# Attention scores of a graph network: the gathered source row is added by TensorE, in place of VectorE

## The chip, the cores and the metric

One core of one Trainium2 chip. The metric is the time on the device of one run of the whole program, in microseconds (us); the kernel before has a median of 9190.53 us over three runs. PE is TensorE, DVE is VectorE, ACT is ScalarE, POOL is GpSimd, SP is SyncE.

## What is computed

Four graph layers run one after the other over 3125 nodes with 64 features and 100,000 edges, each followed by a layer norm. The change touches the last, which holds two GATv2 layers (5 heads of 64 channels). Each does, per edge from `src` to `dst`:

```python
xl = (x @ Wl + bl).reshape(n_nodes, H, C)
xr = (x @ Wr + br).reshape(n_nodes, H, C)
e = jax.nn.leaky_relu(xl[src] + xr[dst], NEG_SLOPE)
alpha = jnp.einsum('ehc,hc->eh', e, att)
# then a softmax of alpha over the edges of one dst, and a sum of a * xl[src]
```

Only the first step of a layer, the scores `alpha` (up to terms that the kernel folds into 2 extra channels a head), is concerned here: `xl[src] + xr[dst]`, 330 numbers an edge (5 heads of 66).

## The kernel before

`gat_edges` (L2229) makes the scores. It is called once for each of the two layers.

**Tiles.** The edges are sorted by `dst` and lie in columns of 128. There are 864 columns (784 of edges and 80 spare ones for columns that cross a boundary). `G = 2` columns are a group, `KC = 12` columns a chunk. One turn of the loop does two chunks, so 24 columns or 12 groups, and there are 36 turns.

**Ahead of the loop** (L2334 to L2347 on PE, with ACT, DVE and SP): for each of 25 blocks of 128 nodes, h is transposed and multiplied in f32 by the two weight matrices (L2344, L2345, 330 columns each). The source part goes to `node_rows` in DRAM (330 numbers and the 64 of h, 1576 bytes a row), the destination part, split in three bf16 terms, to `xr3` and then as a whole into `parts` in SBUF.

**In the loop**, each engine runs its own list of instructions and waits on semaphores:

- POOL (L2321 to L2329) gathers the source rows: one indirect DMA for each column, 128 rows, into `rows`, which has 4 slots of 6 columns (3 groups). Before a slot it waits for its indices (`index_in`), for its release by DVE (`used`) and for SP's store of it (`stored`). Each gather raises `got` of its slot.
- SP loads the row numbers for ACT (L2285) and POOL's next indices (L2290), and stores the h part of each slot to `x_src` (L2296), all in one order written out by hand.
- ACT makes the one-hot matrix of a chunk in two operations (L2384, L2387). The second waits until PE has finished the chunk that used the same buffer (`made`), and raises `hot_made`.
- PE (L2350 to L2361) makes the destination part: for each column one bf16 product of the one-hot matrix with `parts`, 330 columns, into one bank of `psZ`. `psZ` has 4 buffers of 2 banks, one buffer a group. PE waits for `prod`, which says that DVE has read the group four back, and raises `made` after a group.
- DVE (L2407 to L2434) does three operations for each group of 2 columns (660 numbers a partition): it adds the gathered source row to psZ, in place (L2416, it waits for `made`, and for `got` at the first group of a slot, and raises `added`); it takes the maximum with 0, times `att`, from psZ into `lz` (L2423, raises `prod`); it sums over the channels (L2429, raises `scored`). The three are staggered: in one pass it adds for group n, multiplies for n - 1 and reduces for n - 2. After the addition of a slot's last group it releases the slot (`used`, L2421). After six groups the sums are copied into `sj` (L2433).

So the order is POOL's gather and PE's product, then DVE's three operations; POOL can be four slots, PE four groups ahead of DVE.

Of the kernel before, what the change touches and what calls it, by code (L numbers as in the profile page):

```python
# [5 lines left out]
P = 128  # L6
# [17 lines left out]
CE = 128  # L24
# [24 lines left out]
ZH = H * ZC  # L49
# [52 lines left out]
class Space:  # L102


    used = {}
# [2125 lines left out]
def gat_edges(nc, g, h, selfs):  # L2231
# [6 lines left out]
    with phase(nc) as s:  # L2238
# [13 lines left out]
        got = [s.pool_sem(g, k) for k in range(SLOTS)]  # L2252
        dve_c, staged, put, parts_in, cleared = (
            s.sem(n) for n in ("dve_c", "staged", "x_put", "parts_in", "cleared"))
        hot_made, made, added, prod, scored, neared = (s.sem(n) for n in ("hot_made", "made", "added", "prod", "scored", "neared"))
        padded, n_turned, n_ready, n_made, n_tab, n_high, n_split = (
            s.sem(n) for n in ("padded", "n_turned", "n_ready", "n_made", "n_tab", "n_high", "n_split"))
        grp = lambda i, n: i * (2 * NG) + (n + 1)
# [6 lines left out]
        with nc.Block() as block:  # L2265
# [66 lines left out]
            def _(pe):  # L2332
# [17 lines left out]
                with pe.Fori(0, NK // 2) as i:  # L2350
                    for n in range(2 * NG):
                        k, m = divmod(n, NG)
                        if m == 0:
                            at = pick((i * 2 + k) * KC)
                            pe.wait_ge(hot_made, i * 2 + k + 3)
                        pe.wait_ge(prod, grp(i, n))
                        for j in range(G):
                            col = m * G + j
                            last = pe.matmul(psZ[:, n % 4, j, 0:ZH], hot[:, k, col * CE:(col + 1) * CE], parts[:, bass.ds(at[col], 1), :].rearrange("p o c -> p (o c)"),  # L2359
                                             start=True, stop=True)  # L2360
                        last.then_inc(made, 1)  # L2361

            @block.scalar
# [26 lines left out]
            def _(v):  # L2390
# [14 lines left out]
                    v.sem_inc(n_split, 1)  # L2405

                def turn(i, last):  # L2407
                    for n in range(2 * NG + 2):
                        if n < 2 * NG:
                            k, m = divmod(n, NG)  # L2410
                            v.wait_ge(made, grp(i, n) + 2 * NG)
                            slot, at = divmod(n, GS)
                            if at == 0:
                                v.wait_ge(got[slot], i * (16 * KS) + 16 * KS)
                            here = psZ[:, n % 4, :, 0:ZH]
                            v.tensor_tensor(here, here, rows[:, slot, at * G:(at + 1) * G, 0:ZH], ALU.add).then_inc(added, 1)  # L2416
                        if 1 <= n <= 2 * NG:
                            q = n - 1
                            v.wait_ge(added, grp(i, q))
                            if q % GS == GS - 1:  # L2420
                                v.sem_inc(used[q // GS], 1)  # L2421
                            v.wait_ge(scored, grp(i, q))
                            v.scalar_tensor_tensor(lz[:, q % 2], psZ[:, q % 4, :, 0:ZH], 0.0,  # L2423
                                                   att.unsqueeze(1).to_broadcast([P, G, ZH]), ALU.max, ALU.mult).then_inc(prod, 1)
                        if n >= 2:
                            q = n - 2
                            k, m = divmod(q, NG)
                            v.wait_ge(prod, grp(i, q) + 4)
                            v.tensor_reduce(sc[:, k, m * G:(m + 1) * G, :], lz[:, q % 2].rearrange("p g (h c) -> p g h c", c=ZC),  # L2429
                                            X, ALU.add).then_inc(scored, 1)  # L2430
                            if m == NG - 1:
                                v.wait_ge(scored, grp(i, q) + 2)
                                c.link(v.tensor_copy(g.sj[:, :, bass.ds((i * 2 + k) * KC, KC)], sc[:, k].rearrange("p j h -> p h j")))  # L2433
# [517 lines left out]
```

## Time and profile before

| | |
|---|---|
| median of 3 runs | 9190.53 us (9164.67 to 9205.76) |
| profiled execution, time | 9157.66 us |
| its span, from the first instruction to the last | 9156.1 us |
| granted TensorE clock over the span | 0.608 |
| share of the span busy: PE, DVE, ACT, POOL | 42%, 58%, 27%, 41% |
| the loop, each of two layers | 1248 us |

The profile is of one execution. Busy time is that of an engine's operations; handing out instructions and waiting are not in it. An operation's row names the line, the output and inputs, the count, the busy time in all and the mean of one in ns, then the engine's idle time just before it and what ended that. "Issue" is time in which an engine waited for nothing that the profile shows. A timeline row has the start in us from the span's start, the length, and in square brackets the idle time before it.

### The profile page before, as it was taken

The numbers are of one execution on the slowest core, as the hardware profiler recorded it, in microseconds if no ns is written. First come the engines' busy times: TensorE is split into PE (matmuls) and PEld (weight loads), VectorE is DVE, ScalarE is ACT, GpSimd is POOL, SyncE is SP. The second block draws the span as 40 slices with busy tenths as digits, with TensorE's granted clock in tenths as the row PEclk, the third lists the DMA queues.
The fourth block names the chain that finished last, engine by engine and source line by source line (L and its number), as shares of the span: only waits on it lengthen the run. The fifth ranks groups of instructions, "written<-read, shape, count | busy, mean of one in ns | idle before, by whom it ended". The sixth has DMA issues, their size and how long they took to land. (4 is left out here: it accounts for less than half of the span.)

```text
span 9156.1 us, 102588 instructions
## 1 busy us (share of the span) xinstructions
PE 3846.7 (42%) x24601; PEld 3085.2 (34%) x24602; DVE 5285.9 (58%) x8989; ACT 2454.3 (27%) x3870; POOL 3780.2 (41%) x4315
## 2 busy tenths in 40 slices
PE   5455555520017881444443232222249522222196
PEld 2444444520017881333333210000048300000186
DVE  5454445569742112444444468888856588888675
ACT  4333333321622221433333221111112111111121
POOL 4444444400020004444444236666625166666261
PEclk8555555555558995666666555555579555555596
DMA  7565556677737881222222366666645477666462
GB/s 291 152 186 174 170 179 186 184 212 194 284 67 266 293 281 52 82 83 80 93 80 81 44 179 183 184 183 184 171 99 132 128 183 185 182 183 183 107 139 69
DMA packets 1551900, 1462.17 MB, mean 160 GB/s; under 512 B 1296593, under 2 KB 1344365, under 8 KB 1535296
## 3 DMA queue, kind: packets, MB, share of 16 engines
q1 hardware_dynamic: 966152, 807.40, 28.8%
q0 software_dynamic: 175712, 462.09, 19.3%
q10 hardware_dynamic: 409944, 191.70, 7.4%
q8 instruction: 28, 0.46, 0.0%
q14 instruction: 64, 0.52, 0.0%
HBM read 1078.30 MB, written 381.40 MB: 159 GB/s over the span
## 5 line engine op out<-in xcount | busy, mean ns | idle before, releaser
L2328 POOL DMA_INDIRECT rows_p<-node_rows,stage_i x1728 | 1637.9, 948 | 1090.7 <-issue 842.8
L2359 PE MATMUL psZ<-parts_r,hot_t 126*128 x1728 | 629.5, 468 | 1948.7 <-issue 966.3
L2359 PEld LDWEIGHTS psZ<-parts_r,hot_t 126*128 126x128 bf16 x1728 | 181.0, 105 | 2398.1 <-issue 2378.1
L715 PE MATMUL psP<-window,pair_hot 128*128 x3136 | 725.6, 420 | 579.4 <-issue 349.9
L790 DVE SCALAR_TENSOR_TENSOR pair_run<-pair_run,same_c,psP 128x64 f32<-128x64 f32 x1568 | 440.1, 281 | 871.9 <-remote 743.4
L2416 DVE TENSOR_TENSOR psZ<-psZ,rows_p 128x660 f32<-128x660 f32 x864 | 724.7, 846 | 357.7 <-issue 236.5
L715 PEld LDWEIGHTS psP<-window,pair_hot 128*128 128x128 f32 x3136 | 690.8, 329 | 626.7 <-issue 626.7
L257 POOL DMA_INDIRECT rows_s<-hpx,stage_i x784 | 748.5, 955 | 264.7 <-issue 242.7
L257 POOL DMA_INDIRECT both<-table,stage_i x784 | 742.9, 948 | 264.0 <-issue 242.6
L2423 DVE SCALAR_TENSOR_TENSOR lz<-psZ,att 128x660 f32<-128x660 f32 x864 | 723.0, 837 | 95.1 <-issue 69.1
L2429 DVE TENSOR_REDUCE sc<-lz 128x10 f32<-128x660 f32 x864 | 711.9, 831 | 59.4 <-issue 45.1
L2685 PE MATMUL ps_steps<-A,xs 128*65 128x125 f32 x5184 | 574.6, 271 | 145.1 <-DMA xs<-x_src 81.0
L2685 PEld LDWEIGHTS ps_steps<-A,xs 128*65 128x65 f32 x5184 | 558.8, 137 | 160.6 <-issue 153.0
L2384 ACT ACTIVATE near<-locs,third 126x1536 bf16<-126x1536 bf16 x144 | 226.8, 1575 | 1289.6 <-DMA locs<-loc_rows 827.6
L1573 PE MATMUL psY<-parts,tile 128*125 128x192 bf16 x5700 | 516.9, 248 | 112.3 <-DVE parts L1613 97.5
L1938 DVE SCALAR_TENSOR_TENSOR gate<-psZ,la 128x256 f32<-128x256 f32 x196 | 82.9, 423 | 803.1 <-ACT la L1877 655.1
L1573 PEld LDWEIGHTS psY<-parts,tile 128*125 128x125 bf16 x5700 | 484.5, 138 | 117.8 <-DVE parts L1613 98.1
L603 ACT ACTIVATE tile<-psA 128x500 bf16<-128x500 f32 x399 | 203.4, 558 | 979.4 <-remote 640.3
L2704 DVE TENSOR_TENSOR A<-hotw,aw 128x3000 f32<-128x3000 f32 x108 | 354.5, 3283 | 172.1 <-PE ps_steps L2685 171.7
L2659 POOL TENSOR_TENSOR acc<-acc,part_w 65x125 f32 x648 | 316.2, 488 | 282.9 <-ACT part_w L2623 189.1
L2387 ACT ACTIVATE hot_t<-near 126x1536 bf16<-126x1536 bf16 x144 | 213.5, 1483 | 793.0 <-issue 584.4
L1835 PE MATMUL psZ<-b,ones 128*128 128x512 bf16 x196 | 94.3, 481 | 720.4 <-ACT bothT L1867 661.1
(523 smaller groups left out, 8016.2 us busy)
## 6 DMA issues: line engine op xcount, KB each, us to landing
tile<-adj SPq DMA_DIRECT2D x228, 781.2 KB, 4.8
x_src<-rows_p SPq DMA_DIRECT2D x288, 192.0 KB
xs<-x_src SPq DMA_DIRECT2D x432, 128.0 KB, 3.1
locs<-loc_rows SPq DMA_DIRECT2D x144, 378.0 KB
hpx<-stage ACTq DMA_DIRECT2D x25, 2048.0 KB
pair_loc<-pair_locs SPq DMA_DIRECT2D x28, 1792.0 KB
window<-hpx SPq DMA_DIRECT2D x196, 256.0 KB
dst_runs<-pair_run SPq DMA_DIRECT2D x28, 1792.0 KB
```

The costliest lines, as they stand in the source:

```text
L257: pool.indirect_dma_start(buf[:, k, j, 0:width] if width == buf.shape[3] else buf[:, k, j, D:2 * D], None, table, bass.IndirectOffsetOnAxi ...
L715: last = pe.matmul(psP[:, n % 2, j * D:(j + 1) * D], hot[:, n % 2, j * CE:(j + 1) * CE], window[:, n % 2, bass.ds(rel[j], 1), :].rearrange ...
L790: v.scalar_tensor_tensor(run[:, k, at, :], run[:, k, at - 1, :] if at else run[:, 1 - k, PC - 1, :], same[:, k, at:at + 1], psP[:, n % 2, ...
L1573: last = pe.matmul(psY[0:TC, k, 0:3 * D], tile[:, k, b, :], parts[:, b].rearrange("p n c -> p (n c)"), start=b == 0, stop=b == NB - 1)
L2328: pool.indirect_dma_start(rows[:, k, j, :], None, g.node_rows, bass.IndirectOffsetOnAxis(stage[:, k, j:j + 1], 0)).then_inc(got[k], 16)
L2359: last = pe.matmul(psZ[:, n % 4, j, 0:ZH], hot[:, k, col * CE:(col + 1) * CE], parts[:, bass.ds(at[col], 1), :].rearrange("p o c -> p (o c)"),
L2416: v.tensor_tensor(here, here, rows[:, slot, at * G:(at + 1) * G, 0:ZH], ALU.add).then_inc(added, 1)
L2423: v.scalar_tensor_tensor(lz[:, q % 2], psZ[:, q % 4, :, 0:ZH], 0.0, att.unsqueeze(1).to_broadcast([P, G, ZH]), ALU.max, ALU.mult).then_inc ...
L2429: v.tensor_reduce(sc[:, k, m * G:(m + 1) * G, :], lz[:, q % 2].rearrange("p g (h c) -> p g h c", c=ZC), X, ALU.add).then_inc(scored, 1)
L2659: pool.tensor_tensor(here, here, part[:, k, j * WC:(j + 1) * WC], ALU.add).then_inc(added, 1)
L2685: last = pe.matmul(slot(k, j), xs[:, k, j, e, 0:D + 1], A[:, k, j * EG + e, :], start=e == 0, stop=e == EG - 1)
L2704: v.tensor_tensor(A[:, k].rearrange("p f (n h) -> p f n h", h=H), hot[:, k].unsqueeze(3).to_broadcast([P, U * EG, WN, H]), aw[:, k].rearra ...
```

## The change

The identity matrix `ident` (128 x 128, f32) is there already. PE now does two products into the same bank for each column: the bf16 one, which starts the sum, and an f32 product of the identity with the gathered row, 330 columns, which adds to it. PE waits for the slot's gathers, in DVE's place. DVE's addition and the semaphore `added` go. DVE's list for a group is then: wait for `made`, release the slot if the group was its last, wait for `scored`, multiply, and reduce for the group before. The stagger is one group less deep.

```diff
-        hot_made, made, added, prod, scored, neared = (s.sem(n) for n in ("hot_made", "made", "added", "prod", "scored", "neared"))
+        hot_made, made, prod, scored, neared = (s.sem(n) for n in ("hot_made", "made", "prod", "scored", "neared"))
...
                         if m == 0:
                             at = pick((i * 2 + k) * KC)
                             pe.wait_ge(hot_made, i * 2 + k + 3)
+                        slot, col_s = divmod(n, GS)
+                        if col_s == 0:
+                            pe.wait_ge(got[slot], i * (16 * KS) + 16 * KS)
                         pe.wait_ge(prod, grp(i, n))
                         for j in range(G):
                             col = m * G + j
-                            last = pe.matmul(psZ[:, n % 4, j, 0:ZH], hot[:, k, col * CE:(col + 1) * CE], parts[:, bass.ds(at[col], 1), :].rearrange("p o c -> p (o c)"),
-                                             start=True, stop=True)
+                            pe.matmul(psZ[:, n % 4, j, 0:ZH], hot[:, k, col * CE:(col + 1) * CE], parts[:, bass.ds(at[col], 1), :].rearrange("p o c -> p (o c)"),
+                                      start=True, stop=False)
+                            last = pe.matmul(psZ[:, n % 4, j, 0:ZH], g.ident[:, :], rows[:, slot, col_s * G + j, 0:ZH],
+                                             start=False, stop=True)
                         last.then_inc(made, 1)
...
                 def turn(i, last):
-                    for n in range(2 * NG + 2):
+                    for n in range(2 * NG + 1):
                         if n < 2 * NG:
-                            k, m = divmod(n, NG)
                             v.wait_ge(made, grp(i, n) + 2 * NG)
-                            slot, at = divmod(n, GS)
-                            if at == 0:
-                                v.wait_ge(got[slot], i * (16 * KS) + 16 * KS)
-                            here = psZ[:, n % 4, :, 0:ZH]
-                            v.tensor_tensor(here, here, rows[:, slot, at * G:(at + 1) * G, 0:ZH], ALU.add).then_inc(added, 1)
-                        if 1 <= n <= 2 * NG:
+                            if n % GS == GS - 1:
+                                v.sem_inc(used[n // GS], 1)
+                            v.wait_ge(scored, grp(i, n))
+                            v.scalar_tensor_tensor(lz[:, n % 2], psZ[:, n % 4, :, 0:ZH], 0.0,
+                                                   att.unsqueeze(1).to_broadcast([P, G, ZH]), ALU.max, ALU.mult).then_inc(prod, 1)
+                        if n >= 1:
                             q = n - 1
-                            v.wait_ge(added, grp(i, q))
-                            if q % GS == GS - 1:
-                                v.sem_inc(used[q // GS], 1)
-                            v.wait_ge(scored, grp(i, q))
-                            v.scalar_tensor_tensor(lz[:, q % 2], psZ[:, q % 4, :, 0:ZH], 0.0,
-                                                   att.unsqueeze(1).to_broadcast([P, G, ZH]), ALU.max, ALU.mult).then_inc(prod, 1)
-                        if n >= 2:
-                            q = n - 2
                             k, m = divmod(q, NG)
```

## Rows read from the trace of the kernel before

**Rows 1.** The page's head: span and busy time of each engine

```profile
span 9156.1 us, 102588 instructions
...
PE 3846.7 (42%) x24601; PEld 3085.2 (34%) x24602; DVE 5285.9 (58%) x8989; ACT 2454.3 (27%) x3870; POOL 3780.2 (41%) x4315
```

**Rows 2.** Windows, the two loops: length, PE, PEld, DVE, ACT, POOL, clock, DMA share, GB/s

```profile
5397.50:6645.50 1248.00, 313.86 (x862) 89.97 (x860) 1016.26 (x1368) 216.01 (x142) 796.53 (x840) 0.50 0.69 180
...
7320.50:8568.80 1248.30, 313.89 (x862) 89.94 (x860) 1016.31 (x1368) 216.02 (x142) 795.88 (x840) 0.50 0.69 180
```

**Rows 3.** Groups by line, first layer, 5351 to 6646 us

```profile
L2328 POOL DMA_INDIRECT rows_p<-node_rows,stage_i x864 | 819.3, 948 | 544.9 <-issue 421.1 <-DVEq L2436 93.8 <-DVEq L2421 28.5
L2416 DVE TENSOR_TENSOR psZ<-psZ,rows_p 128x660 f32<-128x660 f32 x432 | 362.3, 846 | 179.8 <-issue 116.3 <-PE psZ L2359 47.2 <-DVE sj L2433 11.4
L2423 DVE SCALAR_TENSOR_TENSOR lz<-psZ,att 128x660 f32<-128x660 f32 x432 | 361.4, 837 | 47.8 <-issue 34.3 <-DVE psZ L2416 12.0
L2429 DVE TENSOR_REDUCE sc<-lz 128x10 f32<-128x660 f32 x432 | 355.9, 831 | 28.8 <-issue 22.5 <-DVE lz L2423 6.3
L2359 PE MATMUL psZ<-parts_r,hot_t 126*128 x864 | 314.7, 468 | 974.4 <-issue 507.1 <-DVE lz L2423 358.3 <-ACT hot_t L2387 108.9
...
L2387 ACT ACTIVATE hot_t<-near 126x1536 bf16<-126x1536 bf16 x72 | 106.7, 1483 | 401.6 <-issue 303.3 <-PE psZ L2359 95.1 <-remote 2.7
```

**Rows 4.** Timeline of DVE, one turn of the first layer's loop

```profile
5628.59 0.84 DVE L2416 TENSOR_TENSOR psZ<-psZ,rows_p 128x660 f32<-128x660 f32 x1
...
5630.84 0.84 DVE L2416 TENSOR_TENSOR psZ<-psZ,rows_p 128x660 f32<-128x660 f32 x1
...
5650.08 0.84 DVE L2416 TENSOR_TENSOR psZ<-psZ,rows_p 128x660 f32<-128x660 f32 x1
...
5652.31 0.84 DVE L2429 TENSOR_REDUCE sc<-lz 128x10 f32<-128x660 f32 x1 [0.52 <-issue]
5653.71 0.85 DVE L2416 TENSOR_TENSOR psZ<-psZ,rows_p 128x660 f32<-128x660 f32 x1 [0.56 <-issue]
...
5661.47 0.85 DVE L2416 TENSOR_TENSOR psZ<-psZ,rows_p 128x660 f32<-128x660 f32 x1 [3.27 <-issue]
```

**Rows 5.** Timeline of POOL: gathers that begin a run

```profile
5401.49 0.95 POOL L2328 DMA_INDIRECT rows_p<-node_rows,stage_i  x1 [19.82 <-DVEq L2421]
...
5628.15 0.94 POOL L2328 DMA_INDIRECT rows_p<-node_rows,stage_i  x1 [5.13 <-issue]
...
5663.29 0.94 POOL L2328 DMA_INDIRECT rows_p<-node_rows,stage_i  x1 [5.11 <-issue]
...
5750.68 0.95 POOL L2328 DMA_INDIRECT rows_p<-node_rows,stage_i  x1 [4.33 <-DVEq L2421]
```

**Rows 6.** Timeline of SP, the same turn

```profile
5638.57 0.45 SPq L2296 DMA_DIRECT2D x_src<-rows_p  x1
...
5648.05 0.70 SPq L2296 DMA_DIRECT2D x_src<-rows_p  x1
```

**Rows 7.** Timeline of PE ahead of the loop, f32 products

```profile
5269.41 1.47 PE L2344 MATMUL psZ<-wA,xT 65*128 65x330 f32 x2 [0.96 <-ACT xT L2369]
5270.67 1.31 PE L2345 MATMUL psZ<-wB,xT 65*128 65x330 f32 x2
5271.77 0.42 PE L2337 MATMUL psZ<-ident,x 128*64 128x128 f32 x1
```

**Rows 8.** Windows of other stages, columns as in rows 2

```profile
8900.00:9000.00 100.00, 96.74 (x877) 93.63 (x876) 71.97 (x36) 29.37 (x141) 53.33 (x110) 1.00 0.64 144
7200.00:7300.00 100.00, 55.34 (x99) 26.80 (x99) 53.65 (x126) 18.48 (x59) 18.93 (x20) 0.50 0.49 162
2900.00:3000.00 100.00, 74.42 (x833) 73.52 (x832) 16.04 (x36) 21.47 (x62) 6.07 (x5) 0.88 0.72 246
```

**Rows 9.** Timeline of PE in the loop, two groups

```profile
5783.99 0.73 PE L2359 MATMUL psZ<-parts_r,hot_t 126*128 x2 [2.73 <-issue]
5787.52 0.73 PE L2359 MATMUL psZ<-parts_r,hot_t 126*128 x2 [2.80 <-issue]
```

## The prediction, written before the changed kernel was run

> **What bounds the kernel now.** Read first the head of the page: a span of 9156.1 us, in which DVE is the busiest engine with 5285.9 us, 58% [rows 1]. That is an average over many stages, and the change touches one loop, run once in each of two layers. So the next view is the busy time by stretch: each loop takes 1248 us, DVE is busy for 1016 of them, POOL for 797, PE for 314 at granted clock 0.50 (its lower level, 1.2 GHz) [rows 2]. All I forecast lies in these 2496 us. The profiled execution took 9157.66 us, 33 us below the median of 9190.53.
>
> The groups by line say what a layer does [rows 3]: 864 gathers on POOL, 864 products on PE, and 432 each of DVE's three operations: the addition that goes (362 us), the product with `att` (361 us), the reduction (356 us). A loop turn holds 24 gathers and 12 groups of two columns; there are 36 turns a layer, so 1248 / 36 = 34.7 us a turn.
>
> Now the timelines. From one addition on DVE to the next is 2.25 us (three operations 0.75 us apart, each 0.84 long by the profile, so they overlap a little) [rows 4]: 12 groups need 27 us, and not 34.7. POOL's 24 gathers from 5628.15 take 30.0 us, to 5658.18 (the next one's start less its idle time) [rows 5], 1.25 us each: also not 34.7. What fills the rest is in both timelines. About 22 us after POOL has resumed (at 5628.15), DVE's operations stop following at 0.75 us and come 1.4 us apart, with idle time laid to "issue" before each; two groups take from 5650.08 to 5661.47, 5.7 us each [rows 4]. In SP's timeline a dispatch takes 0.70 us at 5648.05, in place of 0.45 ten us before [rows 6]. I call this a starved stretch: the engines' sequencers hand out an instruction per 0.70 us. POOL, at most four slots of six columns ahead, meets a slot that DVE hasn't released and stops for 5.11 us [rows 5]; 3.3 us after POOL's last gather DVE is regular again, and POOL resumes. So the loop is limited by DVE's speed inside and outside these stretches, with POOL's 30.1 us as the next limit close below.
>
> **What the change takes away.** 432 additions a layer. While regular, a group costs DVE two operations: 2 x 0.75 = 1.5 us in place of 2.25, 18 us a turn. Nothing else in the loop could then use 34.7 us but PE. POOL's floor: in the first layer it resumes at 5401.5 [rows 5] and has 840 gathers left, 840 x 1.25 = 1050 us, then some 15 us for the last slot, so an end at 6467 in place of 6645: 178 us a layer, 355 in all. That is the most that can be won. DVE's counter `added` and its wait go too. `used` is raised right after `made`, earlier than now: worth nothing by itself, since POOL waits for it only when DVE is behind. The reduction follows one group behind and not two: it waits for the product just issued. Such waits stand as 6.3 us a layer in its row today [rows 3]; I take 0, with a bound of 0.1 us a group.
>
> **What it adds to PE.** Two f32 products a group, 330 columns each, with the identity as weights. The nearest rows are the f32 products of 330 columns ahead of the loop: 1.26 us to the next pair's start, and 1.10 to the one after [rows 7]. So a group costs 2 x (0.26 + 1.10) = 2.7 us, at most 3.0, at 1.2 GHz, against 0.5 now (two bf16 products start 0.26 us apart: 0.73 for both less 0.47 for one [rows 3, 9]). At the upper level, 2.4 GHz, the last layer's f32 sums (L2685) have 877 instructions of 125 columns in 96.74 us of busy time at clock 1.00 [rows 8], 0.110 us each; a product is two of them, 330/125 as long: 0.58 us, and a group 2 x (0.13 + 0.58) = 1.4 us. Which level counts? A window with PE busy 55% had 0.50, those with 74% and more had 0.88 and 1.00 [rows 8]. After each pause PE has three slots of backlog and would run without a gap, so I take 4 us at 2.75 us a group and then DVE's 1.5. The Trainium skill, "TensorE: Matmul & The Clock Gate", Part 1, says activity releases a throttle that is on by default; by that rule PE would be quick in its backlog and the time would be my forecast's, while at 1.2 GHz throughout it would be rival 2's. The trace agrees with it in the windows at 74% and 97%.
>
> The larger price is in dispatch. PE's group grows from two weight loads with products to six (an f32 product is two: "x2" in [rows 7]). In a long starved stretch PE's groups came 3.5 us apart (5783.99 to 5787.52) [rows 9], 33 us into a POOL run that began at 5750.68 [rows 5], against 2.25 for a regular group. Whether PE was starved there itself or only waited for DVE the profile does not say ("issue"). Bounds for PE's new group in a stretch: 2.7 us if it isn't starved; 3.5 x 3 = 10.5 us if each load with its product costs as much as there. Inside, 3.5 plus four pairs at one 0.70 each is 6.3, at two 0.70 each 9.1. I take 7.5, nearest to the former.
>
> The new wait for `got` stands on PE ahead of the wait for `prod` and both products. Behind it are only the group's own products, then ACT's next one-hot tile (it waits for `made`), which has 402 us of idle time before its 72 [rows 3]. DVE waited for the same landing so far, so I price the move at 0.
>
> **The sum.** A cycle runs from one resumption of POOL to the next; POOL's lead goes from 9 groups to 12, then it stops. It gains 1/2.51 = 0.398 groups per us. First a check on the kernel before: 20 us regular give 8.9 groups, then 5.7 us a group. 0.398 L = 3 + 8.9 + (L - 20)/5.7 gives L = 37.7 us with 15 groups; the pause, until a slot of 3 groups is free, is 3.3 us (0.6 group) and 2.4 x 2.25 = 5.4. 46.4 us for 15 groups are 37.1 us a turn, against 34.7 measured: right in kind, 2.4 too much. After: 4 us give 1.5 groups, 16 more 10.7, together 12.2, then 7.5 us a group: L = 47.3 with 18.8 groups; pause 3.3 + 2.56 x 2.75 = 10.3; 57.6 us for 18.8 groups are 36.8 a turn. With 6.3 it is 36.2, with 9.1 37.2. So -0.3 us a turn (-0.9 to +0.1) x 72 = -20 us, with the ends -65 and +7; the error of the check is larger than these ends, so this case's own range is 9080 to 9290. Against the median: 9157.66 - 20 + 33 = about 9170; with the lost lookahead (up to 0.1 x 864 = 86 us, mostly covered) I say 9180. The saving on DVE outside the stretches is paid back inside them on PE.
>
> **Rival 1, POOL paces the loop.** PE is never starved, or the stretches depend on DVE's additions and shrink with them. DVE then has two thirds of its instructions in a stretch, 3.8 us a group; L = 74 us, 32.8 us a turn, -300 us; without stretches -355. Time 8835 to 8890. For it: 358 us of PE's idle time a layer are laid to DVE's product, as of an engine that only waits [rows 3], and DVE's regular turn was already below POOL's. Against: POOL would run longer without a pause, and the stretches begin when it does. Chance 0.27. The Trainium skill, "Runtime: NRT & Kernel Launch", Instruction fetch mechanics, gives PE four times the instruction store of the others, and by that PE would hold its loop and this rival would win; no row here shows the store.
>
> **Rival 2, slower: PE becomes the bound outside the stretches too.** If the pauses keep PE at 1.2 GHz, a group costs 2.75 us all the time and 20 us yield 7.3 groups. With 7.5 us in the stretch L = 28.8, 11.5 groups, pause 10.3: 40.8 us a turn, +3.7 against the check, +270 us; with 9.1 it is 41.5, +320. Time 9460 to 9510. It decides from about 1.7 us a group outside the stretches, where the same sum gives 37.4. For it: clock 0.50 in the whole loop today [rows 2], and 55% of busy f32 work didn't lift it [rows 8]. Against: the backlog. Chance 0.23. A worse form, pauses too short to end a stretch (the trace leaves open how short that is), is 12 x 3.8 = 46 us a turn; chance 0.07, beyond my range.
>
> **The numbers.** Forecast case 0.43. A measurement of this kernel can tell about 0.5%, 46 us, from no change. Faster: 0.27 and 0.14 of the forecast case, 0.41; within: 0.18; slower: 0.23, 0.07 and 0.11 of the forecast case, 0.41. The range must reach rival 1's upper half and most of rival 2: 8850 to 9480. The forecast case's own is 9080 to 9290.
>
> **What would show it.** Right: both loops near 1248 us; DVE busy falls by some 360 us a layer; in the stretches PE's groups 6 to 9 us apart while DVE waits for psZ; POOL's pauses fewer and longer, behind runs over 40 us; a granted clock between 0.5 and 0.9. Rival 1: loops of 1070 to 1100 us, POOL without pauses. Rival 2: clock 0.50, PE busy over 85%, DVE waiting for psZ everywhere, loops near 1380 us. The rest of the span should not move; if it does by over 20 us, or if the stretches are gone, my reasoning on dispatch is wrong.

## The result, and the profile after

The changed kernel is slower, by 0.9%: 9269.58 us (median of four runs, 9262.73 to 9277.67) against 9186.76 for the kernel before (four runs, the three of the table and one more), ratio 1.0092, 95% interval 1.0071 to 1.0113. The profiled execution's head, and its two loops (columns as in [rows 2]):

```profile
span 9261.2 us, 108278 instructions
...
PE 4732.9 (51%) x28057; PEld 3751.7 (41%) x28058; DVE 4661.3 (50%) x8125; ACT 2454.4 (27%) x3870; POOL 3778.5 (41%) x4315
```

```profile
5437.00:6714.00 1277.00, 755.64 (x2586) 424.48 (x2585) 703.46 (x935) 214.10 (x140) 795.17 (x840) 0.79 0.68 176
7393.30:8673.70 1280.40, 753.57 (x2585) 423.21 (x2583) 701.68 (x935) 214.08 (x140) 794.04 (x840) 0.79 0.68 175
```

Against [rows 2], DVE's busy time fell by 313 us a loop, PE's rose by 442, and the loop got 29 to 32 us longer. No engine is near full: PE is busy 59% of it, POOL 62%, DVE 55%. The groups by line of the first layer and its waits show where DVE's time went:

```profile
L2328 POOL DMA_INDIRECT rows_p<-node_rows,stage_i x864 | 817.9, 947 | 585.3 <-issue 388.6 <-DVEq L2417 102.4 <-DVEq L2432 94.3
L2364 PE MATMUL psZ<-rows_p,ident 128*128 128x330 f32 x1728 | 723.9, 511 | 0.0
L2419 DVE SCALAR_TENSOR_TENSOR lz<-psZ,att 128x660 f32<-128x660 f32 x432 | 361.9, 844 | 611.8 <-remote 490.2 <-PE psZ L2364 79.3 <-issue 14.2
L2425 DVE TENSOR_REDUCE sc<-lz 128x10 f32<-128x660 f32 x432 | 355.3, 829 | 0.0
L2362 PE MATMUL psZ<-parts_r,hot_t 126*128 x864 | 299.7, 347 | 566.6 <-DVE lz L2419 410.7 <-issue 105.9 <-ACT hot_t L2392 49.5
```

```profile
DVE lz L2419 <- remote: 490.2, 71, 12.3
PE psZ L2362 <- DVE lz L2419: 410.7, 67, 12.4
```

In [rows 3] DVE's idle time was mostly "issue", 116, 34 and 22 us ahead of its three operations. Now it waits 490 us for a signal from another engine ("remote": the profile shows that a signal ended the wait, but no operation that sent it just then), up to 12.3 us at a time, while PE waits 411 us for DVE. One such stall, on DVE, on PE and on POOL:

```profile
6076.71 0.85 DVE L2419 SCALAR_TENSOR_TENSOR lz<-psZ,att 128x660 f32<-128x660 f32 x1 [1.12 <-PE psZ L2364]
...
6079.20 0.22 DVE L2429 COPY sj<-sc 128x60 f32 x1 [0.15 <-DVE sc L2425]
6090.17 1.60 DVE L2419 SCALAR_TENSOR_TENSOR lz<-psZ,att 128x660 f32<-128x660 f32 x2 [10.75 <-remote]
```

```profile
6064.48 0.45 PE L2362 MATMUL psZ<-parts_r,hot_t 126*128 x1 [9.59 <-DVE lz L2419]
6064.73 1.30 PE L2364 MATMUL psZ<-rows_p,ident 128*128 128x330 f32 x2
...
6067.20 0.48 PE L2362 MATMUL psZ<-parts_r,hot_t 126*128 x1
...
6072.08 0.30 PE L2362 MATMUL psZ<-parts_r,hot_t 126*128 x1
...
6073.48 0.30 PE L2362 MATMUL psZ<-parts_r,hot_t 126*128 x1
6073.62 0.72 PE L2364 MATMUL psZ<-rows_p,ident 128*128 128x330 f32 x2
...
6077.70 0.31 PE L2362 MATMUL psZ<-parts_r,hot_t 126*128 x1 [1.15 <-issue]
...
6078.55 0.72 PE L2364 MATMUL psZ<-rows_p,ident 128*128 128x330 f32 x2
6091.15 0.45 PE L2362 MATMUL psZ<-parts_r,hot_t 126*128 x1 [11.89 <-DVE lz L2419]
```

```profile
6064.50 0.94 POOL L2328 DMA_INDIRECT rows_p<-node_rows,stage_i  x1 [4.52 <-issue]
...
6085.77 0.95 POOL L2328 DMA_INDIRECT rows_p<-node_rows,stage_i  x1 [0.30 <-issue]
6091.99 0.95 POOL L2328 DMA_INDIRECT rows_p<-node_rows,stage_i  x1 [5.28 <-DVEq L2417]
```

POOL resumes at 6064.50 and PE does eight groups (16 columns) until 6079.3; by its rows it is four groups ahead of DVE. Yet DVE sees none of these four before 6090.17, when the signals of all four arrive within 0.23 us and PE and POOL go on. POOL's last gather had begun at 6085.77. So the `made` signals of four groups arrive together, about 3 us after POOL's run of 18 gathers is over. The engines wait in a ring: DVE for PE, PE for DVE, POOL for DVE's release of a slot.

This is not the starved dispatch of [rows 4]. I counted the sequencers' own instructions (register, branch and semaphore instructions) that take 0.6 to 0.8 us, in the window of the first loop: in the kernel before 343 on DVE, 25 on PE and 352 on SP; in the changed one none on DVE, none on PE and 207 on SP. SP is still slow in the stall, by its timeline:

```profile
6079.33 0.70 SPq L2285 DMA_DIRECT2D locs<-loc_rows  x1
```

PE has 122 records in the 14.8 us from POOL's resumption to the stall, and none is such a dispatch. The last of its four groups must wait for DVE's product of 6076.71, which ends at 6077.56, and begins at 6077.70: PE's sequencer was at work then, and what DVE lacks is the signals.

The profiled spans differ by 105 us, the loops by 61. The remainder, 44 us, is over the 20 us that I had set as a sign against my reasoning. Most of it, 38 us, lies ahead of the first loop, in stages whose code is the same in both kernels, and their end moves without the change too: the four kernels of the first batch below, all with this code there, begin the loop between 5423 and 5442 us. So I don't lay it to the change; the loops alone explain the difference of the medians, 83 us, to 22.

### The profile page after: what moved, and what is told of

Same layout as the page of the kernel before. It is cut to its first block and busy times, and to the rows that moved or that the text cites. A ratio compares the mean times of both kernels' runs of the same rounds, so it can differ in the third digit from the quotient of the medians.

```text
span 9261.2 us, 108278 instructions
## 1 busy us (share of the span) xinstructions
PE 4732.9 (51%) x28057; PEld 3751.7 (41%) x28058; DVE 4661.3 (50%) x8125; ACT 2454.4 (27%) x3870; POOL 3778.5 (41%) x4315
## 5 line engine op out<-in xcount | busy, mean ns | idle before, releaser
L2364 PE MATMUL psZ<-rows_p,ident 128*128 128x330 f32 x3456 | 1445.6, 510 | 0.0
L2362 PE MATMUL psZ<-parts_r,hot_t 126*128 x1728 | 599.2, 347 | 1137.7 <-DVE lz L2419 868.8
L2364 PEld LDWEIGHTS psZ<-rows_p,ident 128*128 128x128 f32 x3456 | 690.4, 225 | 331.2 <-issue 328.8
L1573 PE MATMUL psY<-parts,tile 128*125 128x192 bf16 x5700 | 518.5, 249 | 113.7 <-DVE parts L1613 97.1
L1573 PEld LDWEIGHTS psY<-parts,tile 128*125 128x125 bf16 x5700 | 485.9, 138 | 119.5 <-DVE parts L1613 97.7
```

The costliest lines, as they stand in the source:

```text
L1573: last = pe.matmul(psY[0:TC, k, 0:3 * D], tile[:, k, b, :], parts[:, b].rearrange("p n c -> p (n c)"), start=b == 0, stop=b == NB - 1)
L2364: last = pe.matmul(psZ[:, n % 4, j, 0:ZH], g.ident[:, :], rows[:, slot, col_s * G + j, 0:ZH], start=False, stop=True)
```

## The experiments

Eighteen experiments in five batches, each batch on one chip of its own with the kernel before timed beside. The batches turned out to be of two kinds, and I speak of two kinds of chips, though no chip served two of these batches: in the first three the kernel before took 9203.8, 9286.2 and 9292.4 us, in the last two 7688.5 and 7696.2. "Loop" is the first layer's, from a window view that begins with DVE's first product with `att`: 1246 us for the kernel before (1248 in [rows 2], with the first addition), 1277 for the changed one. Averages over runs of gathers are counted from the first loop's trace. The kernel before was traced only once, ahead of these batches, and the changed one in the result and in the last batch, so a difference of loops often crosses chips; the ratios do not. An edit that is given for both kernels is shown for one.

### Take the parts apart

No product in the place of the addition; then the product cut to 66 columns:

```diff
-                            pe.matmul(psZ[:, n % 4, j, 0:ZH], hot[:, k, col * CE:(col + 1) * CE], parts[:, bass.ds(at[col], 1), :].rearrange("p o c -> p (o c)"),
-                                      start=True, stop=False)
-                            last = pe.matmul(psZ[:, n % 4, j, 0:ZH], g.ident[:, :], rows[:, slot, col_s * G + j, 0:ZH],
-                                             start=False, stop=True)
+                            last = pe.matmul(psZ[:, n % 4, j, 0:ZH], hot[:, k, col * CE:(col + 1) * CE], parts[:, bass.ds(at[col], 1), :].rearrange("p o c -> p (o c)"),
+                                      start=True, stop=True)
```

```diff
-                            last = pe.matmul(psZ[:, n % 4, j, 0:ZH], g.ident[:, :], rows[:, slot, col_s * G + j, 0:ZH],
+                            last = pe.matmul(psZ[:, n % 4, j, 0:66], g.ident[:, :], rows[:, slot, col_s * G + j, 0:66],
```

> The kernel after without the f32 product with the identity: the gathered source row is not added at all, everything else (waits, stagger, gathers, stores) stays. DVE keeps two operations a group, 1.5 to 1.7 us, PE one product a column. Theory T (the f32 products that read the gathered rows have their completion held back while POOL's gathers run, and DVE idles 10 to 12 us twice a turn for it): the 10 us idle times on DVE are gone, POOL paces the loop with few pauses, each loop 1080 to 1130 us in place of 1277, the whole 8880 to 8970 us. Theory R1 (the loop is limited by starved dispatch or by the gathers' DMAs whatever PE does): loops stay at 1230 to 1280 us, the whole 9180 to 9270 us. Theory R2 (the lost group of stagger and the moved wait for the gathers cost what was lost): also 1230 or more.

Measured: ratio to the kernel before 0.9936 (0.9919 to 0.9952), loop 1222 us. **Taking 362 us of work a layer off DVE and putting nothing in its place wins 24 us.** Theory T, which asked for 1080 to 1130, falls; R1 (1230 to 1280) is near. Its window, and DVE's timeline in a stretch:

```profile
5432.00:6654.00 1222.00, 323.93 (x861) 92.48 (x858) 708.92 (x934) 215.52 (x141) 796.69 (x840) 0.50 0.71 184
```

```profile
6043.30 0.85 DVE L2417 SCALAR_TENSOR_TENSOR lz<-psZ,att 128x660 f32<-128x660 f32 x1 [1.38 <-issue]
...
6047.55 0.85 DVE L2417 SCALAR_TENSOR_TENSOR lz<-psZ,att 128x660 f32<-128x660 f32 x1 [2.02 <-issue]
...
6053.24 0.85 DVE L2417 SCALAR_TENSOR_TENSOR lz<-psZ,att 128x660 f32<-128x660 f32 x1 [3.46 <-issue]
```

Groups come 4.3 and 5.7 us apart, much as in [rows 4], though DVE has two operations a group. POOL, kept waiting less, makes longer runs: 22.7 gathers on average against 16.9 before, and the stretch lasts as long as the run. That is what becomes of a faster DVE here. Starved dispatch is back without the f32 product, on PE too: counted as above, 448 on DVE and 551 on PE.

> The kernel after with the identity product cut to the first 66 of 330 columns of each gathered row, so 4/5 of the source row are not added. PE has the same number of instructions and the same waits; the f32 product's time in the array falls from about 0.70 us (2.4 GHz) or 1.38 us (1.2 GHz) a column of edges to about a fifth. Theory T (completion of products that read the rows is held back while gathers run, whatever their size): loops 1240 to 1280 us as in the kernel after. Rival, array time (PE at 2.7 us a group at 1.2 GHz after each wait is what is too slow): loops fall to 1080 to 1150 us, the whole to 8880 to 9020 us. Rival, dispatch of six weight loads and products a group: the count is unchanged, so loops stay near 1277 us and PE's groups stay late.

Measured: ratio 1.0031 (1.0021 to 1.0041), loop 1260 us, with DVE again waiting 387 us for "remote":

```profile
5442.00:6702.00 1260.00, 573.11 (x2586) 505.02 (x2585) 702.13 (x934) 215.55 (x141) 795.22 (x840) 0.51 0.69 178
```

The rival of array time alone, 1080 to 1150, falls. So the two f32 products a group, four instructions as the program writes them (two loads, two products, each shown twice), cost 38 us by being there (1222 to 1260, both in this batch), and only 17 by their other 264 columns (1260 to 1277). The clock was 0.51 here and 0.79 in the changed kernel, so the 17 us are the price as the two ran, not at one clock.

### The moved wait, and the DMA traffic

The kernel before with only the wait for `got` moved to PE; the changed kernel with one column of six in SP's store to `x_src`:

```diff
+                        if col_s == 0:
+                            pe.wait_ge(got[slot], i * (16 * KS) + 16 * KS)
                         pe.wait_ge(prod, grp(i, n))
...
-                            if at == 0:
-                                v.wait_ge(got[slot], i * (16 * KS) + 16 * KS)
```

```diff
-                                 rows[:, k, :, ZH:TR]).then_inc(stored[k], 16)
+                                 rows[:, k, 0:1, ZH:TR]).then_inc(stored[k], 16)
```

> The kernel before with one part of the change alone: the wait for a slot's gathers moved from DVE to PE, ahead of the bf16 products. DVE still adds. Theory T: without products that read the rows nothing is held back; loops 1245 to 1260 us, the whole within 0.4% of the kernel before. Rival, the moved wait (PE can no longer work ahead of the gathers, so each landing is followed by PE's latency before DVE starts, and four made signals come at once after it): loops 1270 to 1290 us and DVE idle times of 5 to 12 us for a remote signal twice a turn, the whole 9230 to 9270 us.

Measured: 0.9983 (0.9972 to 0.9994), loop 1241 us. The wait costs nothing on PE; the move even wins a little. DVE hands out fewer instructions, which may be why; that wasn't tested.

> The kernel after with SP's store of the h part cut from six columns of a slot to one (5/6 of x_src are not written). The gathers, their count and their waits are unchanged; the store's packets (768 a slot, 256 bytes each) fall to 128. Theory T in the form that the DMA traffic beside the gathers is what delays: loops shrink to 1150 to 1230 us and the idle times of DVE shorten. If only the gathers themselves matter, or PE's speed: loops within 10 us of 1277.

Measured: 1.0063 (1.0042 to 1.0084), loop 1278 us. The store isn't the cause.

Then both kernels with gathers of 128 numbers a row in place of 394:

```diff
-                            pool.indirect_dma_start(rows[:, k, j, :], None, g.node_rows,
+                            pool.indirect_dma_start(rows[:, k, j, 0:128], None, g.node_rows.rearrange("a c -> (a c)")[0:NR * 128].rearrange("(a c) -> a c", c=128),
```

> The kernel before with each gather moving 128 numbers of a row (512 bytes) in place of 394 (1576 bytes), from a contiguous part of the same table; the rest of the rows is zero. POOL issues the same 864 gathers a layer of 128 rows each at 1.25 us, DVE and PE do the same work. Theory S1 (the starved stretches come from the bytes that the gathers move): no stretches, loops fall to POOL's 1085 us or a little above, the whole to 8870 to 8920 us. Theory S2 (they come from the gathers' issue and descriptors, 128 rows at a time, whatever their size): stretches of 0.70 us a dispatch still begin about 18 us after POOL resumes and loops stay within 15 us of 1248.

> The kernel after with the same narrowed gathers. Under S1: no stretches, PE and DVE both below POOL's pace, loops 1080 to 1110 us, equal to the narrowed kernel before within 20 us, so the change gains nothing even then. Under S2 loops stay at 1260 to 1285 us. If PE's f32 work is a bound of its own (2.7 us a group at 1.2 GHz): loops about 1150 to 1200 us with clock 0.5 and PE busy over 80%.

Measured: the kernel before 0.9994 (0.9979 to 1.001), loop 1254; the changed one 1.0056 (1.0036 to 1.0076), 1279 us from its first product with `att` to its last. The window of the first:

```profile
5508.00:6762.00 1254.00, 312.44 (x856) 89.09 (x856) 1013.16 (x1365) 214.18 (x141) 793.75 (x840) 0.50 0.35 88
```

DMA share 0.35 in place of 0.69, 88 GB/s in place of 180, and the same time and stretches. The bytes aren't the cause. What stays the same is that POOL issues 864 gathers of 128 rows.

### What PE is given in the product's place

Two more bf16 products a column; or, with no product, counter increments on PE, four a column:

```diff
-                            last = pe.matmul(psZ[:, n % 4, j, 0:ZH], g.ident[:, :], rows[:, slot, col_s * G + j, 0:ZH],
+                            pe.matmul(psZ[:, n % 4, j, 0:ZH], hot[:, k, col * CE:(col + 1) * CE], parts[:, bass.ds(at[col], 1), :].rearrange("p o c -> p (o c)"),
+                                      start=False, stop=False)
+                            last = pe.matmul(psZ[:, n % 4, j, 0:ZH], hot[:, k, col * CE:(col + 1) * CE], parts[:, bass.ds(at[col], 1), :].rearrange("p o c -> p (o c)"),
```

```diff
+                            for q in range(4):
+                                pe.sem_inc(pad, 1)
```

> The kernel after with the f32 identity product of each column replaced by two more copies of the bf16 product (so the source row is not added and the destination part counts three times). PE has the same number of weight loads and products a group as with the f32 product, six of each, but reads nothing of the gathered rows and each product takes a bf16 pass. Known by now: without any product in its place a loop is 1219 us, with the f32 product cut to 66 columns 1259, uncut 1277. If the number of instructions that PE must be handed is what costs (dispatch in the stretches): loops 1250 to 1265 us. If it is the f32 data or the reading of the gathered rows: loops 1215 to 1235 us.

Measured: 1.012 (1.0091 to 1.0149), loop 1303 us, above both forecasts. That is longer than with the f32 products (in the same batch, with the narrow gathers: 1.0056 and 1279), though PE's busy time fell to 558 us and no product reads the gathered rows. DVE waits 461 us for "remote", so the late signals don't need such a product.

```profile
5511.00:6814.00 1303.00, 557.88 (x2585) 268.68 (x2583) 701.86 (x935) 214.66 (x141) 795.59 (x840) 0.71 0.66 172
```

> The kernel after with the f32 product taken out (the source row is not added) and eight instructions of PE's sequencer alone (counter increments) a group in its place, as many as the f32 product has weight loads and matmul passes. Known by now: without anything in its place a loop is 1219 us; with the identity product cut to 66 columns 1259; uncut 1277; with two more bf16 products in its place 1300. If what costs is the number of instructions that PE's sequencer has to be handed while POOL's gathers run: loops 1250 us or more. If it is the weight loads and products themselves: loops 1215 to 1230 us.

Measured: 1.0318 (1.0294 to 1.0343), loop 1343 us and 1386 (products with `att`, first to last) in the second layer. **Eight counter increments a group, which do nothing in the array, cost more than the f32 products.** Whether each costs as any instruction, or as an increment, no run separates. The window, then PE's timeline; POOL's run had begun at 5928.86:

```profile
5507.00:6850.00 1343.00, 388.84 (x862) 89.65 (x861) 706.41 (x935) 215.35 (x141) 796.22 (x840) 0.50 0.64 167
```

```profile
5935.85 0.45 PE L2363 MATMUL psZ<-parts_r,hot_t 126*128 x1 [0.37 <-issue]
5936.60 0.45 PE L2363 MATMUL psZ<-parts_r,hot_t 126*128 x1 [0.30 <-issue]
5941.07 0.43 PE L2363 MATMUL psZ<-parts_r,hot_t 126*128 x1 [4.01 <-issue]
5945.35 0.44 PE L2363 MATMUL psZ<-parts_r,hot_t 126*128 x1 [3.85 <-issue]
5946.36 0.45 PE L2363 MATMUL psZ<-parts_r,hot_t 126*128 x1 [0.58 <-issue]
```

One product with its load, address and four increments takes 0.75 us, and from about 8 us into POOL's run 4.3 us; about 3 us after the start of the run's last gather (5942.65) it is quick again. Counted in the first loops' traces, from POOL's resumption to an engine's first dispatch of about 0.70 us (medians, which move by some 10% with the bounds of "about"): here PE, 60 instructions in 7.8 us; before, DVE, 50 to 55 in 18 to 20 us; without product, DVE 60 in 19 to 20 and PE 80 to 87 in 17 to 20 us. So the start of a stretch isn't a fixed time after POOL resumes: in these three kernels, the more instructions an engine uses per us, the sooner it comes. The changed kernel isn't among them, nor are those with 66 columns or two more bf16 products: none has such a dispatch on PE or DVE.

### Pace POOL

Both kernels with POOL waiting after every 12 gathers until they have landed; then with a memset of 1.4 us in its place (in the kernel before, together with the moved wait). The first edit is the kernel before's; in the changed one POOL waits for the second and fourth slot alone:

```diff
+                        if k == 2:
+                            for q in range(2):
+                                pool.wait_ge(got[q], i * (16 * KS) + 16 * KS)
...
+                    for q in range(2, 4):
+                        pool.wait_ge(got[q], i * (16 * KS) + 16 * KS)
```

```diff
+                        if k % 2 == 0:
+                            pool.memset(idle[:, :], 0.0).then_inc(paused, 1)
+                            pool.wait_ge(paused, i * 2 + k // 2 + 1)
```

> The kernel before with POOL waiting, after every 12 gathers, until these have landed. A burst is 15 us and the wait 3 to 4 us, so POOL can't give more than a turn of 36.5 to 38 us, loops 1315 to 1370 us, the whole 9330 to 9440 us. What it tells: if the stretches come from a gather run of over 18 us, there are none, DVE's additions are never 'issue'-starved and DVE waits for POOL; if 0.70 us dispatches still appear, they come from something else than the length of the run.

Measured: 1.0058 (1.004 to 1.0075), loop 1280 us, where I had expected 1315 to 1370. DVE's groups by line:

```profile
L2421 DVE TENSOR_TENSOR psZ<-psZ,rows_p 128x660 f32<-128x660 f32 x431 | 361.8, 847 | 256.5 <-DMA rows_p<-node_rows,stage_i 247.9 <-issue 2.4 <-DVE sj L2438 1.4
L2428 DVE SCALAR_TENSOR_TENSOR lz<-psZ,att 128x660 f32<-128x660 f32 x432 | 360.6, 835 | 1.2
L2434 DVE TENSOR_REDUCE sc<-lz 128x10 f32<-128x660 f32 x432 | 355.1, 829 | 0.0
```

With runs of 15 us, DVE's idle time by "issue" falls from 173 us ([rows 3]) to 2.4. The stretches do need long gather runs; but the pauses cost more than they save.

> The kernel after with POOL waiting, after every 12 gathers, until these have landed (the same pacing took the kernel before to loops of 1275 us and left no starved dispatch). If DVE's idle times of over 6 us (54 in the first loop, 534 us in all) come from PE being held back while a run of gathers is under way, they are nearly gone, and the loop is POOL's alone: 36 turns of two times 15 us and two waits of 3.3 us, 1275 to 1320 us, the same as now though the stalls are away. If the stalls come from PE itself (clock, f32 passes), they stay and add to it: 1350 us or more.

Measured: 1.0079 (1.0053 to 1.0106), loop 1280 us. "Remote" ahead of DVE's product falls from 490 to 19 us, as expected, and DVE waits 407 us for PE, PE 450 us for the gathers: POOL sets the time. DVE's idle times over 8 us, 28 in the changed kernel's first loop, are gone, and the loop is as long as with them. (Over 6 us I now count 43 there after the loop's start, 372 us in all, not the 54 and 534 of the expectation.)

> The kernel after with a fixed pause on POOL after every 12 gathers, a memset of 1.4 us of a tile that nobody reads. POOL can then give a turn in 33 us at best. If a short pause suffices to let the others catch up: loops 1190 to 1230 us, the whole below the kernel before by 0.3 to 1%. If the pause must last until the gathers have drained (about 3 us, as the ends of the stalls suggest): runs are still cut by waits for released slots and loops stay at 1260 to 1300 us.

> The kernel before with the wait for the gathers moved to PE (which alone gave loops of 1238 us) and the same fixed pause of 1.4 us after every 12 gathers. Same alternatives: 1200 to 1225 us if a short pause suffices, 1235 to 1270 if not.

Measured: the changed kernel 1.0055 (1.0037 to 1.0073), loop 1267; "remote" is still 382 us, so 1.4 us don't suffice. The kernel before with both edits: **0.9975 (0.9963 to 0.9986)**, loop 1236. That is the best complete version here, faster than both kernels by little. The moved wait alone had 0.9983 in another batch, and the two intervals overlap: that the pause adds anything isn't shown.

### Other chips

Half as many increments on PE (two increments a column, no product), a fixed column of `parts` for the bf16 product, and the kernel before with groups of three columns:

```diff
-                            pe.matmul(psZ[:, n % 4, j, 0:ZH], hot[:, k, col * CE:(col + 1) * CE], parts[:, bass.ds(at[col], 1), :].rearrange("p o c -> p (o c)"),
+                            pe.matmul(psZ[:, n % 4, j, 0:ZH], hot[:, k, col * CE:(col + 1) * CE], parts[:, col % NWR, :],
```

```diff
-    G = 2
+    G = 3
...
-        psZ = s.ps("psZ", [P, 4, G, 512])
+        psZ = s.ps("psZ", [P, 2, G, 512])
```

> As the kernel with eight counter increments a group on PE, but with four: no f32 product, 11.75 instructions of PE a group. Theory N (the number of instructions that PE's sequencer is given decides): loops between the 1219 us of none and the 1342 to 1386 of eight, 1265 to 1300 us. If the eight crossed a limit that four don't reach: loops 1215 to 1230 us.

> The kernel after with each bf16 product reading a fixed column of the destination table in place of the one picked at run time (so the destination part is that of other nodes). All weight loads, all f32 and bf16 products and all waits stay; gone are PE's load of 12 numbers a chunk and the two register operations a group that make the addresses, 2.3 of 15.8 records of PE a group. Theory N: loops shorter than 1277 us by 15 to 30 us. Rival (PE's weight loads and products, their array time or clock): loops 1270 to 1280 us, no change.

> The kernel before with groups of three columns in place of two (psZ two buffers of three banks) and the wait for the gathers on PE. DVE's operations are 8 times three a turn of 990 elements in place of 12 times three of 660, so DVE hands out about 55 instructions a turn in place of 80 and PE about 80 in place of 94; DVE's busy time falls only by the operations' fixed part. PE has one buffer of lead less. Theory N: stretches begin later or not at all; loops 1130 to 1200 us, the whole below the kernel before by 0.9 to 2.3%. Rival (the loop is limited by the gather runs and their pauses whatever the others' instruction counts): loops 1230 to 1250 us. If two buffers are too few: DVE waits for PE at every group, loops 1240 to 1300 us without starved dispatch.

Measured: 0.9987 (0.9978 to 0.9997), 1.0003 (0.9994 to 1.0013) and 1.0035 (1.0023 to 1.0048). All three expectations presupposed stretches, and there were none on this chip: the kernel before took 7688.5 us. The latter two were run again, beside the changed kernel, and fell on another such chip:

> The changed kernel as it is, beside the kernel before on the same chip. On a chip where dispatch is starved: ratio 1.005 to 1.012, loops 1265 to 1290 us. On a chip without starved stretches (the kernel before at about 7690 us): POOL paces both kernels, loops 1060 to 1070 us, ratio 0.998 to 1.003, although DVE has a third less to do.

Measured: **1.0010 (1.0000 to 1.0019)**, loop 1071 us. Its window, two of its groups by line, and SP's timeline:

```profile
4294.00:5365.00 1071.00, 751.56 (x2587) 425.20 (x2585) 703.77 (x935) 214.03 (x141) 795.35 (x840) 0.86 0.80 210
```

```profile
L2328 POOL DMA_INDIRECT rows_p<-node_rows,stage_i x840 | 795.4, 947 | 278.9 <-issue 244.4 <-DVEq L2417 29.6 <-DMA x_src<-rows_p 4.9
...
L2419 DVE SCALAR_TENSOR_TENSOR lz<-psZ,att 128x660 f32<-128x660 f32 x432 | 365.3, 846 | 405.2 <-PE psZ L2364 386.1 <-DVE sj L2429 3.0
```

```profile
4602.34 0.45 SPq L2296 DMA_DIRECT2D x_src<-rows_p  x1
...
4632.36 0.45 SPq L2296 DMA_DIRECT2D x_src<-rows_p  x1
```

POOL's 840 gathers with 0.30 us between two take nearly all of the loop; no "remote" is left in DVE's row and SP's dispatch stays at 0.45 us, where [rows 6] had 0.70. PE does all f32 work in 1071 us with time to spare.

> The changed kernel with a fixed column of the destination table in place of the one picked at run time (the destination part is then that of other nodes); 2.3 of 15.8 records of PE a group are gone, all weight loads and products stay. On a chip with starved stretches, if the number of instructions of PE's sequencer decides: loops 15 to 30 us shorter than the changed kernel's of the same chip, 1245 to 1262. If PE's loads and products decide: within 8 us of it. On a chip without stretches: 1060 to 1070 us.

> The kernel before with groups of three columns, two buffers of psZ and PE waiting for the gathers. On a chip with starved stretches, if the numbers of instructions decide: stretches later or gone, loops 1130 to 1200 us, the whole 0.9 to 2.3% below the kernel before. If the gather runs and pauses decide whatever the counts: 1230 to 1250 us. On a chip without stretches: 1065 to 1072 us and a ratio of 1.002 to 1.005, as it was there.

Measured: 1.0003 (0.9993 to 1.0012) and 1.0034 (1.0021 to 1.0046). In all of these POOL makes its 840 gathers in one run without a pause: its pace is the limit, and an edit on PE or DVE changes little. Why groups of three cost 0.3% is open.

## Why the prediction was wrong

It said "no change, or a little less" (9180, own range 9080 to 9290); the result is 83 us above the kernel before. It lies inside the own range too, but that is luck: the range was as wide as the error of my check, and what happened in the loop is something else than its middle describes. From 1246 to 1277 us a loop the account is: DVE's addition away and the stagger and waits changed, -24; two f32 products a group as instructions, +38; their other columns in the array, +17; together +31. The 38 was measured within one batch; the other two terms take one loop from there and one from the traces shown with the result. Whole runs of the first batch say the same of the first two: -28 and +40 a loop.

- **The failed step is the cycle of the sum: "4 us give 1.5 groups, 16 more 10.7, together 12.2, then 7.5 us a group".** It let DVE go on for 20 us after POOL resumes and at a slower pace after that, POOL running 47 us with a pause of 10.3. Measured, nothing reaches DVE in the stall at all: in the stall shown DVE stops 14.8 us after POOL resumes, after eight groups of PE (the median over its 43 idle times of more than 6 us in the first loop is 15.3), and goes on some 3 us after POOL's last gather. POOL's runs shrank to 15.4 gathers (19 us), with pauses of 4.1 on average. Of "-0.3 us a turn" came +0.9.
- **The mechanism in that step was wrong too.** I priced PE's groups in a stretch by starved dispatch. With the eight increments PE does starve, about 8 us into a run. In the changed kernel no dispatch of PE or DVE is slow: by its rows PE finishes its four groups of lead and then waits for DVE, while the `made` signals come late and together. So PE's groups are not 6 to 9 us apart; DVE waits for signals, up to 12.3 us at a time.
- **The gain on DVE was oversized.** By the same sum, a DVE without the addition and with no starved PE (rival 1's form with stretches) gives 300 us in two layers. The experiment gave 56 by the medians. I had the reason among those against rival 1, POOL would run longer without a pause, and didn't carry it through: what DVE gains outside a stretch, POOL's lead turns into a longer stretch.
- **Right:** the saving on DVE is paid back on PE, and more by what PE is handed (38) than by the columns (17). That this is dispatch, as I said, isn't shown. The prices of a group, 1.4 and 2.7 us, stand in the rows: 1.40 us from 6072.08 to 6073.48, and 2.72 from 6064.48 to 6067.20, right after a pause. The clock was 0.79, between 0.5 and 0.9 as I said; the rule that I cited from "TensorE: Matmul & The Clock Gate" in the Trainium skill, Part 1, agrees with these rows, where a first product takes 1.30 us after 9.59 us of idle time and later ones 0.72. DVE's busy time fell by 313 us in the window, not 360: its two other operations overlap less.
- **The moved wait at 0 was right** (1241 against 1246 us, ratio 0.9983). The shallower stagger, also priced at 0, wasn't tried alone.
- **Rival 1** holds where dispatch isn't starved: POOL paces the loop at 1071 us, as I worked out (1070 to 1100). It gives no gain there, since the two kernels take the same time: the addition costs nothing under POOL's pace. **Rival 2** fell: PE is busy 59%, at clock 0.79.
- I weighed the rule of the Trainium skill, "Runtime: NRT & Kernel Launch", Instruction fetch mechanics, by which I took PE to hold its loop. The runs are divided on it: without the product and with the increments PE is slowed after 60 to 87 instructions, as soon as DVE or sooner; in the changed kernel it isn't. Rival 1, which I tied to it, didn't win on the chip of the result either way.

Open: why PE's `made` signals come together after a run in the changed kernel, when its rows show the groups done; whether the array's work is late and its rows early, or only the signals are, the profile can't say. So the cause of the 38 us is known as far as this: it comes with the added instructions on PE, and on chips without stretches it is gone. Also open is whether the loop follows the count of instructions in steps as small as two a group: all runs for that fell on chips without stretches.

## What to carry to other kernels

When busy engines all stand at 50 to 60% and idle time is "issue" or "remote" on several engines at once, look at the number of instructions and not only at microseconds: an engine's slack in busy time doesn't show that it can take more of them, and here one on DVE became four on PE. Look at the dispatches themselves as well: in the changed kernel none on PE or DVE was slow, and the time was lost in signals that came late. Before trading work between engines, run the kernel with the work simply left out: here that shows 24 us of 1246 to be won. And look at whether the time depends on the chip; a gain or loss measured under starved dispatch may vanish on the next one.

## What was not expected of the hardware

- The unchanged kernel took 9187 to 9292 us in the result and three batches, and 7689 and 7696 in two others, each on a chip of its own. In these the trace of the changed kernel shows no dispatch of 0.70 us; DVE's operations (846 ns) and gathers (947 ns, 1.25 us apart) are as long as before. Nearly the whole difference, 1527 of 1556 us between the two traces of the changed kernel, lies in the four stages with hundreds of indirect gathers each: 1662 us became 1099, 1554 became 1010, and the two loops 206 and 214 us less. A stage of matrix products with 15 gathers in all (L1573) took 671 and 672.
- Dispatch on DVE, PE or SP falls to 0.70 us in long runs of indirect gathers, whatever the gathers' size: 88 or 180 GB/s gave 1254 and 1246 us. In runs of 12 gathers with a wait for the landing no dispatch of DVE or PE did.
- Eight counter increments a group (1343 us, ratio 1.0318) cost more than four bf16 products (1303, 1.012), and these more than two f32 products (1277, 1.0092; in the bf16 products' batch, with narrow gathers, 1.0056), each ratio against the kernel before of its own batch.
- Four of PE's signals can reach DVE within 0.23 us, some 3 us after a run of gathers, when PE's rows show the last of their groups done 11 us earlier.
